# A graph-and-LSTM layer on one core: unread float32 matmuls between stages, and recurrent matmuls whose columns are streamed eight times

## The reference

```python
xn = _layernorm(x)
x = x + gnn(xn, src, dst, ...) + mix(xn[None], ...)[0]
x = x + ffn(_layernorm(x)[None], ...)[0]
# in ffn: x_proj = x @ W_ih.T + b_ih + b_hh
def step(carry, xp):
    h, c = carry
    gates = xp + h @ W_hh.T
    i, f, g, o = split(gates, 4)
    c = sigmoid(f) * c + sigmoid(i) * tanh(g)
    h = sigmoid(o) * tanh(c)
    return ((h, c), h)
# then: logits of h, gate = argmax, w = gate * h,
# out = 2 h + prefix_sum(w) * fw_att + suffix_sum(w) * bw_att
```

## Time and profile before

| | |
|---|---|
| median of 3 runs | 16,084.2 us (16,082.2 to 16,095.2) |
| profiled execution | 16,096.5 us, span of the trace 16,094.8 |
| TensorE matmul busy | 12,549.7 us, 78% |
| TensorE weight load busy | 11,596.3 us, 72% |
| VectorE busy | 10,109.2 us, 63% |
| ScalarE busy | 5,158.2 us, 32% |
| GpSimd busy | 2,040.0 us, 13% |
| mean granted TensorE clock | 0.544 |

### The profile page before, as it was taken

How to read it: one execution, slowest core, us unless ns; L and a number is a source line. 1 busy time by engine, 2 the same in 40 slices (tenths; PEclk the granted TensorE clock), 3 DMA queues, 4 the chain that set the end, 5 groups by cost and what they waited for, 6 DMA issues and landing times. The chain is left out here.

```text
span 16094.8 us, 920575 instructions
## 1 busy us (share of the span) xinstructions
PE 12549.7 (78%) x375284; PEld 11596.3 (72%) x375284; DVE 10109.2 (63%) x84155; ACT 5158.2 (32%) x32368; POOL 2040.0 (13%) x1573
## 2 busy tenths in 40 slices
PE   3444446888888888888888888888888888888887
PEld 2333334788888888888888888888888888888886
DVE  4443222666666666666666666666666666666667
ACT  1111111333333333333333333333333333333333
POOL 5887885000000000000000000000000000000000
PEclk8666777555555555555555555555555555555556
DMA  6555554100000000000000000000000000000000
GB/s 169 90 91 84 83 83 99 67 2 2 2 2 2 2 2 2 2 2 2 2 2 2 2 2 2 2 2 2 2 2 2 2 2 2 2 2 2 2 2 17
DMA packets 622798, 340.12 MB, mean 21 GB/s; under 512 B 455829, under 2 KB 571433, under 8 KB 622134
## 3 DMA queue, kind: packets, MB, share of 16 engines
q0 software_dynamic: 150048, 204.90, 7.9%
q1 hardware_dynamic: 461968, 129.69, 3.9%
q10 hardware_dynamic: 10742, 5.06, 0.1%
HBM read 172.29 MB, written 160.65 MB: 21 GB/s over the span
## 5 line engine op out<-in xcount | busy, mean ns | idle before, releaser
L1363 PE MATMUL bank<-hrest,whh 128*128 128x1 bf16 (+1 forms) x300000 | 9080.9, 166 | 1920.2 <-DVE hrest L1487 1920.2
L1363 PEld LDWEIGHTS bank<-hrest,whh 128*128 128x128 bf16 x300000 | 8555.7, 104 | 2483.1 <-DVE hrest L1487 2482.7
L1431 ACT ACTIVATE gates<-bank 128x4 f32<-128x4 f32 x12500 | 2198.1, 176 | 8137.1 <-DVE bank L1468 7260.1
L1468 DVE TENSOR_REDUCE bank<-bank 128x4 f32<-128x12 f32 x12500 | 2212.9, 177 | 3178.9 <-PE bank L1363 2296.2
L1363 PE MATMUL bank<-xsteps,wih 128*128 128x15 bf16 (+1 forms) x60048 | 2715.4, 174 | 0.0
L1476 DVE CUSTOM_DVE_ANT_1 uv<-gates 128x4 f32<-128x4 f32 x12500 | 2041.6, 163 | 445.9
L1363 PEld LDWEIGHTS bank<-xsteps,wih 128*128 128x128 bf16 x60048 | 2278.7, 103 | 0.0
L1439 ACT ACTIVATE bank<-gates 128x1 f32<-128x1 f32 x12500 | 2188.1, 175 | 119.3
L1492 DVE TENSOR_TENSOR hrest<-hrest 128x1 f32<-128x1 f32 x12500 | 1993.3, 159 | 216.2
L1497 DVE TENSOR_TENSOR hrest<-hrest 128x1 f32<-128x1 f32 x12500 | 1981.5, 159 | 217.3
L1363 PE MATMUL bank<-ones,gbias 128*128 128x5 bf16 x10008 | 1679.9, 168 | 9.7 <-DMA xsteps<-x_d 9.7
(11 more groups left out here) (167 smaller groups left out, 3295.4 us busy)
## 6 DMA issues: line engine op xcount, KB each, us to landing
acc_d<-zero SPq DMA_DIRECT2D x40, 640.0 KB, 12.6
ht<-acc_d SPq DMA_DIRECT2D x100, 224.0 KB
xsteps<-x_d SPq DMA_DIRECT2D x1252, 15.0 KB, 1.7
U<-hrest SPq DMA_DIRECT2D x1250, 5.0 KB, 1.7
x_d<-x SPq DMA_DIRECT2D x25, 750.0 KB, 3.2
rows<-xn_d,staged_i POOLq DMA_INDIRECT x782
acc_d<-sums,target POOLq DMA_INDIRECT x782, 3.8
xi<-xn_d SPq DMA_DIRECT2D x50, 125.0 KB
```

The costliest lines, as they stand in the source:

```text
L1363: return nc.tensor.matmul(to, w, v, start=start, stop=True, skip_group_check=True)
L1431: nc.scalar.activation(gates[:, k, 0:2 * NG_[k]:2], zi[k], ACT.Tanh).then_inc(ifg_act[k], 1)
L1468: nc.vector.tensor_reduce(zi[k], gi[k][b][:, s], axis=AX.X, op=ALU.add).then_inc(ifg_summed[k], 1)
```

## The change

It has two parts. The first is a helper `keep_running`, which issues float32 matmuls of 512 columns with the identity as weights into bank 7; nothing reads what they write. Five of them stand behind the nodes' last `layer2`, three at the head of the norm stage's TensorE program, ahead of its first wait, and eight at the head of the LSTM's, ahead of its first wait. The second lets each recurrent matmul of the LSTM stream its one to three columns eight times (`WIDE = 8`), by a moving operand that is repeated with a step of zero. The output has eight places instead of one: the first is where the gates lay before, the other seven lie behind it in the same bank and are not read. The projection's matmuls stay as they are.

```diff
+AFTER_NODES, BEFORE_NORM, BEFORE_STEPS = 5, 3, 8
+WIDE = 8
...
+def keep_running(nc, count, to, w, v):
+    for _ in range(count):
+        nc.tensor.matmul(to, w, v, start=True, stop=True, skip_group_check=True)
...
                 layer2(NC - 1, (NC - 1) % 2)
+                keep_running(nc, AFTER_NODES, bank[7][:], ident[:], U[:, 0, 0:512])
...
             def _(pe):
+                keep_running(nc, BEFORE_NORM, bank[7][:], ident[:], U[:, 0, 0:512])
                 pe.wait_ge(avg_ready, 1)
...
+            gi_wide = [[bank[2 * k + b][:, 0:WIDE * B * NG_[k] * PARTS]
+                        .rearrange("p (r t g c) -> p t g r c", r=WIDE, t=B, c=PARTS) for b in range(2)] for k in range(KD)]
+            go_wide = [bank[4 + b][:, 0:WIDE * B * PARTS].rearrange("p (r t c) -> p t r c", r=WIDE, t=B) for b in range(2)]
...
             def _(pe):
+                keep_running(nc, BEFORE_STEPS, bank[7][:], ident[:], XT[:, 0, 0:512])
                 pe.wait_ge(lstm0, 1)
...
+                    def streamed(k, p):
+                        return hpart[:, 0:PARTS - p, before, k].rearrange("p (r c) -> p r c", r=1)\
+                            .broadcast_to([128, WIDE, PARTS - p])
...
-                            last = matmul(gi[m][b][:, s, g, 0:PARTS - p], whh[:, p, k, cols],
-                                          hpart[:, 0:PARTS - p, before, k], False)
+                            last = matmul(gi_wide[m][b][:, s, g, :, 0:PARTS - p], whh[:, p, k, cols], streamed(k, p), False)
...
-                        return matmul(go[b][:, s, 0:PARTS - p], whh[:, p, k, cols],
-                                      hpart[:, 0:PARTS - p, before, k], False)
+                        return matmul(go_wide[b][:, s, :, 0:PARTS - p], whh[:, p, k, cols], streamed(k, p), False)
```

## The result

| | before | after |
|---|---|---|
| median | 16,084.9 us (16,082.2 to 16,095.2) | 16,215.3 us (16,214.8 to 16,225.4) |
| ratio | | 1.0082, 95% interval 1.0069 to 1.0095 |
| profiled execution | 16,096.5 us, span 16,094.8 | 16,225.4 us, span 16,223.6 |
| mean granted TensorE clock | 0.544 | 0.544 |

One slip in the text ahead of the prediction: the projection's 520 columns per five steps are streamed by 56 matmuls (eight gate blocks, one bias and six products each); 104 is the number of its columns per step. The prediction's sums use the 104 columns and stay as they are.

A forecast was written before the change was run, and what follows sets the result against it. Bound by the LSTM's 6,250 serial steps of 2.06 us, a ring without slack. 131 + 5.4 - 1 = +135 us gave 16,220 us on the median (forecast 0.60); range 16,080 to 16,700.

The forecast's parts named there:

- The ring and its 21 ns: LSTM step loop, 30th matmul through half 0's state to next step: no slack, 21 ns longer, 131 us (109 to 144).
- The spacing: LSTM's 48 recurrent matmuls: starts stay 27 ns apart, since 24 columns occupy the array for only 20 ns.
- Neither adds anything: LSTM matmuls ending half 1 and the output gate: also move 21 ns, but half 0 already shifted the whole step.
- the warm rival: LSTM: clock kept at 2.4 GHz through the steps, about 15,590 us; chance 0.15.
- The term on which everything hung: LSTM: granted clock falls back within the first steps and stays at 0.50 for the 12.9 ms.
- the comparison of columns per us: TensorE: changed steps stream 423 per us, below the norm stage's 523 at 0.50; logits stream 1,170 at 1.00.
- The first rival's price: LSTM at 2.4 GHz: each step 0.08 us shorter, 500 us in all, about 15,590 us; chance 0.15.
- the matmul's own time besides its columns: Float32 records: 170 ns at 1.00, 245 at 0.50, giving up to 0.07 us more per LSTM step at full clock.
- The second rival: LSTM's eightfold output slower than a column per cycle: 16,385 us at 1.5 cycles, 16,880 at two; chance 0.15.
- Head: Eight unread calls ahead of the LSTM steps delay the first projection to 3039.4: +5.4 us.
- Nodes' end: Ten unread records behind the last `hid,gw` matmul: 4.3 us, hidden behind VectorE's chain with half a us to spare.
- Norm: Three unread calls at the norm stage's head: -1 us taken, bounds +2.6 to -40; clock expected at 0.50 again.

The follow-up runs named there:

- wide_near: Changed kernel without the unread float32 rows, the eight places of a gate behind each other instead of 60, 45 or 15 apart: 16,198.6 us, ratio 1.0066.
- ends_42: Changed kernel without the unread rows, only the 42nd recurrent matmul (last of half 1's gates) streaming eight times: 16,191.9 us, ratio 1.0069.
- all_but_one: Changed kernel without the unread rows, 47 of 48 recurrent matmuls streaming eight times, the 30th once: 16,203.8 us, ratio 1.0073.
- wide_only: Changed kernel without the unread rows at the three places, all recurrent matmuls still eightfold: 16,223.1 us, ratio 1.0084.
- hold_24: Like `hold_clock`, but gate runs of 24 places at most and three unread matmuls of 288 instead of 224 columns: 16,059.0 us, ratio 0.9977.
- hold_clock: Changed kernel with neighbouring runs of 24 or 33 places, 30th, 42nd, 48th matmuls narrow, three unread 224-column matmuls per step: 16,427.9 us, ratio 1.0209.
- warm_wide: Changed kernel plus projection matmuls streamed four, six and eight times and three unread 352-column bf16 matmuls per step: 17,862.9 us, ratio 1.1109.

## Why the prediction was right

**The ring and its 21 ns.** Predicted 21 ns a step and 131 us; the distance from the 30th to the sum grew by 21 ns, the step by 19.6, 122.5 us. The lower bound of the term, a cycle a column (17.5 ns), is what 21 columns cost when they are written in a row (`wide_near`, 16.9); the eight places apart add 4 ns. The value of 21 was a choice between 17.5 and 23 that leaned on the slope of the earlier trace rows. That this slope held the cost of the broken pattern as well is likely, but no run shows it, so that the choice met the number so well is in part luck.

**The spacing.** Said to stay at 27 ns with 24 columns, and it did.

**"Neither adds anything".** This step was wrong, though the sum didn't suffer. I had written that the ends of half 1 and of the output gate add nothing, since half 0 already shifts the whole step. `ends_42` shows that the 42nd alone costs 0.69%. There are two rings of nearly the same length, and the cost is not twice 21 ns because they run beside each other, not because half 1 has slack. The trace of before had it in view: I noted in the warm rival that the third part of half 1 and the 27th matmul "arrive nearly together", and did not draw from it that half 1 is a ring of its own. Whoever had acted on the prediction and narrowed only the 30th matmul would have won some 20 us of 139 (`all_but_one` against `wide_only`). For the output gate the step holds: its sum starts 28 ns later than the 48th matmul would let it.

**The clock.** The term on which everything hung was called right: 1.00 for two steps, then 0.50. The reason given for it, the comparison of columns per us, was not shown. The rule of the Trainium skill, TensorE: Matmul & The Clock Gate, section Why this matters for your kernels, that the full clock is kept unless idle gaps come between bursts, is not what these traces show: the stage came in at 1.00, no gap in a step was over 0.4 us, and it fell; in `hold_24` the granted clock fell in a microsecond in which matmuls ran without a gap (3498 to 3499), with 0.03 us of idle time in the 3 us before. The logits, with matmuls in only 41 of 70 us, stayed at 1.00. The kernels that held the clock closed their gaps and streamed more columns at the same time (in `hold_24` matmul busy in 12,783 of 12,800 us), so no run here says which of the two held it.

**The first rival's price.** It didn't come, but its price was mis-sized: 0.08 us a step and 500 us for the full clock, where `hold_24` measured 6 to 10 ns and some 40 us. The term that failed is the matmul's own time besides its columns, 245 ns at 0.50 and 170 at 1.00 by float32 rows of 250 columns. The bf16 matmuls of the steps don't have it: 15 columns last 180 ns at 0.50 and 179 in `hold_24` at 1.00, and the distance from the 30th to the sum is 204 ns at either. I had carried a difference from one kind of matmul to another.

**The second rival.** At 24 columns it isn't there at 1.2 GHz, as forecast. Its mechanism is, further on: with 31 to 33 repeated columns the distance of starts is 30 to 33 ns at full clock (`hold_clock`). The Trainium skill, PSUM — Partial Sum Buffer, section Specifications (TRN2), says that a non-contiguous pattern slows a matmul considerably. What the runs show of it is graded: 4 ns at 24 columns in eight places (`wide_only` against `wide_near`), hidden in the spacing and seen only by who waits; 58 ns on average between the starts of matmuls of 40 and 60 columns in runs of up to three (`warm_wide`), in which the repetition of the input has a share that I can't separate from the places of the output.

**The rows.** Head: 5.4 us predicted, 5.7 measured from the block's opening, with the first projection at 3039.28 for 3039.4. Nodes' end: hidden, as said, with 0.4 us to spare. Norm: -1 predicted, -0.6 between the two traces, and of that size in the other kernels with these rows.

## What to carry to other kernels

In a chain of short matmuls, what a column costs is decided by who waits for it: 45 of 48 matmuls took eight times the columns for 0.1% together, and any one of the two that close a ring cost 0.7%. Ahead of counting a loop's slack from the wait that is listed, look for a second value that is used just when it gets ready, and for idle time too short to be listed: with two rings of nearly equal length, mending one of them won 20 us of 139. Before paying for a clock, measure what it gives to the work on the path: here twice the clock made matmuls with 1 to 24 columns start no closer, and was worth 0.2%. And look at the clock in short stretches: a mean of 1.00 hid 35 falls.

## What the runs showed of the chip

- Weight load and bf16 matmul with 1 to 24 columns start 26 to 27 ns apart at a granted clock of 0.50 and at 1.00 alike.
- The engine that waits for such a matmul starts 204 ns after its start with three columns, and 0.8 ns later for each further column: 211 at 12, 221 at 24 in a row, 225 at 24 in eight places. At 1.00 it is 204 with three columns and 222 with 24 in eight places: the 21 columns cost 17.6 ns instead of 20.8. Why that doesn't halve with the clock's cycle is open.
- At 1.00, neighbouring columns of an unrepeated bf16 operand cost 0.42 ns each (352 in 149 ns, 224 in 95); 31 to 33 columns of the state, repeated, took about 1 ns each, even where they were written in a row. Whether it is the repetition or that the state's bf16 values are the upper halves of float32 values, and so not neighbours, was not tried apart.
- Full clock took 7 ns off the distance from the first matmul after a wait to the second (47 ns before, 40 in `hold_24`).
- The granted clock can fall with no idle time on TensorE: in `hold_24` from 1.00 to 0.50 within 3498 to 3499 us, matmul busy all of it, and back by 3502.
